# A graph network on one core: segment sums transposed unmerged, messages in partition quarters, each block added at its own base

## What is computed

```python
W   = (edge_attr @ ew + eb).reshape(E, 16, 16)      # 8 features an edge
msg = einsum('ei,eio->eo', x[src], W)
agg = segment_sum(msg, dst, num_segments=N)         # N = 12500
h   = agg + x @ rw + rb
```

## Time and profile before

| | before |
|---|---|
| median of three runs | 7843.1 us |
| profiled execution | 7844.6 us, span 7842.8 us |
| mean granted TensorE clock | 0.978 |
| TensorE matmuls busy | 94% |
| DVE busy | 75% |
| POOL busy | 68% |
| ScalarE busy | 64% |

### The profile page before, as it was taken

One profiled execution on the slowest core, in us unless ns is written; L12 is line 12 of the kernel. 1 busy time (PEld: TensorE's weight loads), 2 busy tenths in 40 slices (PEclk: granted clock), 3 DMA queues, 4 the chain that ended last, 5 costly groups with the idle time before them and its releaser, 6 DMA issues.

```text
span 7842.8 us, 135584 instructions
## 1 busy us (share of the span) xinstructions
PE 7377.1 (94%) x51692; PEld 6562.7 (84%) x51692; DVE 5875.9 (75%) x7566; ACT 5020.2 (64%) x8367; POOL 5324.6 (68%) x5635
## 2 busy tenths in 40 slices
PE   4999999999999899999999999999999999999998
PEld 2888888888888688888888888868888888888887
DVE  3777777777777677777777777767777777777775
ACT  3666666666666466666666666656666666666665
POOL 4677777777777377777777777737777777777772
PEclk7999999999999799999999999989999999999998
DMA  7111111111111111111111111111111111111110
GB/s 37 29 30 30 30 30 30 30 30 30 30 28 29 26 30 30 28 30 30 30 30 30 30 30 30 29 25 29 30 30 30 30 27 30 30 30 30 30 30 20
DMA packets 783265, 229.16 MB, mean 29 GB/s; under 512 B 643869, under 2 KB 733869, under 8 KB 782619
## 3 DMA queue, kind: packets, MB, share of 16 engines
q1 hardware_dynamic: 529252, 172.27, 10.7%
q0 software_dynamic: 180000, 46.44, 6.9%
q10 hardware_dynamic: 73367, 1.76, 1.0%
HBM read 216.52 MB, written 3.52 MB: 28 GB/s over the span
## 4 chain that ended last, share of the span: by engine, by line
PE 66%; ACT 28%; issue 2%; DVE 2%; DMA 1%; DVEq 1%; ACTq 0%
PE bank L1074 57%; ACT distance L914 13%; ACT low_hot L918 13%; PE bank L1088 2%; PE bank L1030 2%; PE bank L1089 2%; ACT z L878 1%; PE bank L1097 1%; PE bank L1098 1%; DMA key_all<-in_src 1%; PE bank L1143 1%; DVE xbig L638 1%; PE bank L1155 1%; DVEq L719 0%; DVE agg L724 0%
## 5 line engine op out<-in xcount | busy, mean ns | idle before, releaser
L468 POOL DMA_INDIRECT xg<-node_table,idx x5625 | 5323.8, 946 | 2394.5 <-issue 1768.1
L1074 PE MATMUL bank<-nodes,low_hot 128*128 128x400 f32 x30000 | 5729.9, 348 | 25.0 <-DVE nodes L651 15.1
L1074 PEld LDWEIGHTS bank<-nodes,low_hot 128*128 128x128 f32 x30000 | 5401.4, 188 | 285.0 <-issue 254.8
L914 ACT ACTIVATE distance<-key_all,low_id 128x640 bf16<-128x640 int16 x3000 | 2242.6, 818 | 2056.8 <-issue 1298.9
L683 DVE TENSOR_TENSOR spread<-mask,bank 128x400 f32<-128x400 uint8 x3750 | 2015.5, 565 | 1571.9 <-PE bank L1074 1571.6
L918 ACT ACTIVATE low_hot<-distance,one 128x640 fp32r<-128x640 bf16 x3000 | 2231.0, 815 | 0.0
L688 DVE TENSOR_REDUCE xg<-spread 128x80 f32<-128x2000 f32 x750 | 1677.3, 2236 | 25.7
L638 DVE TENSOR_TENSOR xbig<-xg,bank 128x1280 f32<-128x1280 f32 x750 | 1327.4, 1810 | 1.0 <-issue 0.2
L1041 PE MATMUL bank<-xbig,hot 128*32 128x144 f32 x18750 | 992.6, 294 | 0.0
L1041 PEld LDWEIGHTS bank<-xbig,hot 128*32 128x32 f32 x18750 | 819.7, 109 | 163.6 <-issue 101.3
L1088 PEld LDWEIGHTS bank<-merge,z 128*128 128x128 f32 x942 | 146.7, 188 | 428.2 <-ACT z L878 422.8
(11 more groups left out here) (109 smaller groups left out, 1031.3 us busy)
## 6 DMA issues: line engine op xcount, KB each, us to landing
key_all<-edge_keys SPq DMA_DIRECT2D x375, 320.0 KB, 3.7
xg<-node_table,idx POOLq DMA_INDIRECT x5625
ea<-in_edge_attr SPq DMA_DIRECT2D x375, 100.0 KB
idx<-in_src SPq DMA_DIRECT2D x375, 7.5 KB
node_table<-rows_room SPq DMA_DIRECT2D x3, 781.2 KB
xbig<-node_table SPq DMA_DIRECT2D x9, 192.0 KB
xbig<-in_x SPq DMA_DIRECT2D x2, 781.2 KB
xbig<-in_dst ACTq DMA_DIRECT2D x1, 782.5 KB, 68.1
```

The costliest lines, as they stand in the source:

```text
L468: pool.indirect_dma_start(out=xg[u][:, j, :], out_offset=None, in_=table[:, :], in_offset=bass.IndirectOffsetOnAxis(ap=idx[u][:, j:j + 1], ...
L914: nc.scalar.activation(distance[f][:, 0:tiles.stop - tiles.start, :], key[u % KEYS][:, tiles, :], ACT.Abs, bias=low_id[:, f:f + 1]).then_i ...
L1074: last = nc.tensor.matmul(p_sel[t % BANKS], low_hot[:, f, t, :], nodes[i][:, f, :, :].rearrange("p d f -> p (d f)"), start=(f, i) == (0, 1 ...
```

## The change

SPAN, SHIFTS, `slide`, `merge`, `set_merges` and the semaphore `s_merge` go, and with them the steps at the start that moved the bases of a round's blocks together. Each block keeps its own base.

```diff
-            base_4 = base_f[:].rearrange("p (r c) -> p r c", c=GANG)
...
-            nc.vector.tensor_copy(base_i[:], base_4[:, :, 0])
...
-            step(nc.vector.tensor_tensor(base_f[:], base_f[:], apart_f, ALU.subtract))
+            nc.vector.tensor_copy(base_i[:], base_f[:, 0:NB])
```

```diff
-                pe.wait_ge(s_merge, n + 1)
...
-                pe.wait_ge(s_add, layer * R + r - r % QROUNDS + CREDIT)
-                nc.tensor.matmul(p_zT, z[r % PAIR][:, D:D + FD], merge[r % SHIFTS][:], start=True, stop=True)
-                nc.tensor.matmul(p_zxT, z[r % PAIR][:, 0:D], merge[r % SHIFTS][:], start=True, stop=True).then_inc(s_T, 1)
+                pe.wait_ge(s_add, layer * NB + (r - r % QROUNDS) * GANG + CREDIT)
+                nc.tensor.transpose(p_zT, z[r % PAIR][:, D:D + FD], ident[:])
+                nc.tensor.transpose(p_zxT, z[r % PAIR][:, 0:D], ident[:]).then_inc(s_T, 1)
```

```diff
+        p_agg = [bank[2][q % GANG * WIN:q % GANG * WIN + D, q // GANG * P:(q // GANG + 1) * P]
+                 for q in range(QROUNDS)]
...
-                nc.tensor.matmul(to, w_now[:], zT[:, 0:count, :].rearrange("p q w -> p (q w)"), start=True, stop=False)
-                nc.tensor.matmul(to, eb_now[:], zxT[:, 0:count, :].rearrange("d q w -> d (q w)"),
-                                 start=False, stop=True).then_inc(s_mm, 1)
+                for first in range(0, count, GANG):
+                    some = range(first, min(first + GANG, count))
+                    for q in some:
+                        nc.tensor.matmul(p_agg[q], w_now[:], zT[:, q, :], start=True, stop=False)
+                    for q in some:
+                        last = nc.tensor.matmul(p_agg[q], eb_now[:], zxT[:, q, :], start=False, stop=True)
+                last.then_inc(s_mm, 1)
```

```diff
-                rounds = quad_rounds(q)
-                bases = [dve.value_load(base_i[0:1, r:r + 1], min_val=0, max_val=N - 1) for r in rounds]
                 dve.wait_ge(s_mm, layer * QUADS + q + 1)
-                for r, base in zip(rounds, bases):
-                    here = agg[:, bass.ds(base, SPAN)]
-                    dve.wait_ge(s_add, layer * R + r + CREDIT)
-                    nc.vector.tensor_tensor(here, here, p_agg[:, r % QROUNDS, :], ALU.add).then_inc(s_add, 1)
+                for r in quad_rounds(q):
+                    blocks = range(r * GANG, min((r + 1) * GANG, NB))
+                    bases = [dve.value_load(base_i[0:1, n:n + 1], min_val=0, max_val=N - 1) for n in blocks]
+                    for n, base in zip(blocks, bases):
+                        here = agg[:, bass.ds(base, WIN)]
+                        dve.wait_ge(s_add, layer * NB + n + CREDIT)
+                        nc.vector.tensor_tensor(here, here, p_agg[r % QROUNDS][:, n % GANG * WIN:(n % GANG + 1) * WIN],
+                                                ALU.add).then_inc(s_add, 1)
```

```diff
                                          bias=low_id[:, f:f + 1]).then_inc(s_dist, 1)
+                if between is not None:
+                    copy_rounds(layer, between)
                 for f in range(FOLD):
...
-                        if g:
-                            copy_rounds(layer, g - 1)
...
-                            compare_keys(layer, b, u + 2, 1)
-                copy_rounds(layer, G - 1)
+                            compare_keys(layer, b, u + 2, 1, between=g)
+                        else:
+                            copy_rounds(layer, g)
```

More of the change, by code:

```diff
@@ L26 @@
 GANG = 4
-SPAN = 100
-SHIFTS = 4
 QUAD = 4
@@ L62, in gnn_kernel @@
     assert E == G * GE and G == BODIES * SLOTS and FD == P and D * (F + 1) <= 512
-    assert GANG * WIN == P and QROUNDS * SPAN <= 512 and FETCHED % RUN == PICKED % RUN == 0 and NB == BLOCKS * G
+    assert GANG * WIN == P and QROUNDS <= 2 * GANG and FETCHED % RUN == PICKED % RUN == 0 and NB == BLOCKS * G
     assert N == NODE_P * PER and PER == CHUNKS * SUB and CHUNKS % SLOTS == 0 and CN <= 512
@@ L122, in gnn_kernel @@
         dst_rel = sb("dst_rel", [P, NB, RUN], I16)
-        base_i = sb("base_i", [P, R], I32)
+        base_i = sb("base_i", [P, NB], I32)
         base_f = sb("base_f", [P, R * GANG])
-        slide = sb("slide", [P, R])
-        merge = [sb(f"merge{i}", [P, SPAN]) for i in range(SHIFTS)]
         far_i = sb("far_i", [P, 1], I32)
@@ L175, in gnn_kernel @@
         z = [sb(f"z{i}", [P, D + FD]) for i in range(PAIR)]
-        zT = sb("zT", [P, QROUNDS, SPAN])
-        zxT = sb("zxT", [D, QROUNDS, SPAN])
+        zT = sb("zT", [P, QROUNDS, P])
+        zxT = sb("zxT", [D, QROUNDS, P])
         low_c = sb("low_c", [G, BLOCKS])
@@ L208, in gnn_kernel @@
         p_z = [bank[i][:, 0:D + FD] for i in range(PAIR)]
-        p_zT, p_zxT = bank[2][:, 0:SPAN], bank[2][0:D, SPAN:2 * SPAN]
-        p_agg = bank[2][0:D, 0:QROUNDS * SPAN].rearrange("d (q w) -> d q w", w=SPAN)
+        p_zT, p_zxT = bank[2][:, 0:P], bank[2][0:D, P:2 * P]
+        p_agg = [bank[2][q % GANG * WIN:q % GANG * WIN + D, q // GANG * P:(q // GANG + 1) * P]
+                 for q in range(QROUNDS)]
         p_far, p_far_agg = bank[0][0:FAR_WIN, 0:D + FD], bank[1][0:D, 0:FAR_WIN]
@@ L269, in gnn_kernel @@
         s_seg = sem("segments_summed")
-        s_merge = sem("merge_onehot_ready")
         s_z = sem("round_copied")
@@ L559, in _ @@
             step(nc.vector.tensor_copy(base_f[:, GANG * G:NB], bank[2][:, P:P + G]))
-            base_4 = base_f[:].rearrange("p (r c) -> p r c", c=GANG)
-            apart_4 = apart_f.rearrange("p (r c) -> p r c", c=GANG)
-            nc.vector.tensor_copy(base_i[:], base_4[:, :, 0])
[L563 to L571, removed]
-            step(nc.vector.tensor_tensor(base_f[:], base_f[:], apart_f, ALU.subtract))
+            nc.vector.tensor_copy(base_i[:], base_f[:, 0:NB])
             step(nc.vector.tensor_tensor(dst_rel[:], dst_at, base_f[:, 0:NB].unsqueeze(2).to_broadcast([P, NB, RUN]),
@@ L746, in segments @@
                         multiply_fetched(layer, b, u)
-                        set_merges(layer, g)
                         if another:
@@ L757, in segments @@
                 add_quad(layer, QUADS - 1)
-                dve.wait_ge(s_add, layer * R + (R + CREDIT))
+                dve.wait_ge(s_add, layer * NB + (NB + CREDIT))
                 apart(dve)
@@ L897, in copy_segments_far, with compare_keys @@
                         nc.scalar.activation(far_zxT[:], p_farxT, ACT.Copy).then_inc(s_fzT, 1)
-            def compare_keys(layer, b, u, half):
+            def compare_keys(layer, b, u, half, between=None):
                 body = layer * BODIES + b + u // SLOTS
@@ L1095, in messages_of @@
                 pe.wait_ge(s_zT, layer * R + rounds[-1] + 1)
-                to = p_agg[:, 0:count, :].rearrange("d q w -> d (q w)")
-                nc.tensor.matmul(to, w_now[:], zT[:, 0:count, :].rearrange("p q w -> p (q w)"), start=True, stop=False)
-                nc.tensor.matmul(to, eb_now[:], zxT[:, 0:count, :].rearrange("d q w -> d (q w)"),
-                                 start=False, stop=True).then_inc(s_mm, 1)
+                for first in range(0, count, GANG):
[5 more added lines that the diff above has]
+                last.then_inc(s_mm, 1)
             def segment_sums(layer):
```

## The result

The changed kernel takes 8598.3 us (8596.3 to 8600.8) where the kernel before took 7842.5 in runs beside it: a ratio of 1.096 (1.0945 to 1.0983). It is slower, as forecast, and lies in the range; the forecast of 8720 was 122 us too high. The profiled execution of after has a span of 8597.0 us and a mean granted clock of 0.904, against 7842.8 us and 0.978.

The account below looks back on a forecast made before the run. TensorE was taken as the bound, waiting for the z copy and DVE's adds. Per layer +423 +19.8 -98.7 -31.3 -18.6 = +294.2; three layers +882.6, start -4.5, on 7844.6 gave 8722.7, said as 8720 us; range 8540 to 8930.

Parts of the forecast that it names:

- The lump: DVE's 20 loads and 20 adds a quad: the products after them start 13.5 us later, rounds of 3.67 us.
- The clock: TensorE at half clock after waiting for the adds: fifth pick tile 5.2 us after them, making 14.1 us late, not 13.5.
- the merge: Merge one-hots removed from DVE's path between the adds and the first taken tile: about 0.25 us less.
- The transposes: On TensorE, two transposes replace two pairs of merging matmuls: -0.25 us a round, bounds -0.1 to -0.35; -31.3 a layer.
- The moved copy: ScalarE copies z before the one-hots, so TensorE's wait goes: -1.05 us in 94 groups a layer, -98.7 a layer.
- The messages: TensorE's message matmuls in four column quarters: -0.6 us, 31 times, -18.6 a layer; bounds -0.85 to +0.5.
- The layer ends: Last group of each layer, where nothing lies beside the adds and five blocks are left over: +19.8 us.
- The start: Removed steps on the bases at the kernel's start: -4.5 us, once.
- Hidden loads: Rival: DVE's sequencer runs all later loads beside the adds; faster, about 7710 us; chance 0.06.
- The dearer clock: Rival: TensorE's clock stays at half for the longest time seen, about +1.6 us more each, 8870 us; chance 0.12.
- the copy gives nothing back: Rival: another wait, DVE's fifth tile or ScalarE's next half, takes TensorE's 1.05 us; 8970 us; chance 0.08.
- cheaper loads: Rival: DVE's value loads are cheaper than now or partly hidden, midway, 8300 us; chance 0.04.

Follow-up runs that it names:

- copy_only: The kernel before with only the z copy moved between ScalarE's distances and one-hots: 7541.4 us, ratio 0.961.
- copy_unmoved: The changed kernel with the z copy put back at its old place after the one-hots: 8894.7 us, ratio 1.134.
- one_load: The changed kernel with one value load a round instead of four, same 20 adds, sums landing on wrong nodes: 7766.8 us, ratio 0.990.
- many_loads: The kernel before with 20 value loads ahead of its five adds, each base loaded four times and one used: 8820.4 us, ratio 1.124.
- keep_busy_2: The changed kernel with TensorE repeating pick tile 2 eight times while it waits for the adds: 8523.6 us, ratio 1.087.
- loads_early_2: The changed kernel with a quad's 20 value loads placed one by one behind earlier takings of pick tiles, where DVE waits: 7788.2 us, ratio 0.993.
- copy_quarters_2: The kernel before with moved z copy and messages in partition quarters, merging matmuls and five adds kept: 7481.0 us, ratio 0.954; on another chip 12190.6 us.

## Why the prediction was right, and by how much not

**The mechanism** held in each step that makes the change slower: value loads of 0.61 us in a row that nothing covers, DVE's lump of adds, TensorE behind it at the transposes, the clock at half after that. copy_only and copy_unmoved fit 7545 and 8895 to within 4 us, one_load and many_loads each show 0.62 us a load, from either side. Of the signs that the prediction named, the loads are there 1875 times at 300 ns, from the first load of a quad to the end of its last add it is 18.1 us (some 18 were forecast), TensorE's wait is 13.3 us (about 14), and the granted clock behind it is 0.50.

**The lump, +13.5 us: measured +13.08** (last add's start 5.58 to 18.66 us, means of 90 quads). A round is 3.60 us in the mean, 3.55 in the quad shown (4054.25 to 4057.78 and so on in DVE's timeline), instead of 3.67: I let the next load begin 0.08 us after the last add began, and it begins after 0.03; from that load to the next add it is 2.61 us where I had 2.65. The last add of round one comes 0.37 us earlier than I said, since the 0.35 us for a long first load, read in one quad, isn't the rule. In the kernel before the same quad misled me the other way: over all quads its first add starts at 4.04 us, in the quad that I read at 4.33. These two slips nearly cancel, which is luck. One quad was taken for all.

**The clock: forecast +0.6 us after 0.25 for the merge, measured 14.27 against 13.69, +0.58**, and by keep_busy_2 0.84 for the clock less 0.26 for the merge one-hots, both as forecast. In the quad shown it is granted 0.50 and 0.82 behind the wait:

```profile
4056.50:4069.60 13.10, 0.19 (x2) 0.00 (x0) 2.96 (x17) 1.27 (x3) 9.99 (x11) 0.60 0.24 41
4069.60:4072.00 2.40, 2.30 (x8) 2.24 (x9) 2.40 (x2) 0.42 (x2) 1.79 (x3) 0.50 0.08 6
4072.00:4074.00 2.00, 2.00 (x11) 1.99 (x10) 2.00 (x4) 0.00 (x0) 1.42 (x2) 0.82 0.07 6
```

Both together: +13.67 instead of +14.1 a quad, 40 us in all.

**The transposes, -0.25 us a round: measured about -0.48** (copy_only 18.01, after 17.54). This is the largest miss, and outside the bounds that I gave, -0.1 to -0.35. I took 0.11 us for each of the two from the earlier trace rows; the pair takes 0.13 together. In the timeline of after the second starts 0.10 us behind the first (4019.74 to 4019.84), and the picks only 0.03 behind the second. So the five transposes of L997 were the right row for the first of the pair and the wrong one for the second, which has 16 stationary columns; why it is so short no run shows. By 94 rounds on the path and the second rounds of 31 groups that is 0.23 x 125 x 3, some 86 us, of the 122.

**The moved copy, -1.05 us:** 1.06 and 1.03. **The messages, -0.6:** -0.55 (1.87 to 1.32). **The layer ends:** +17 to +20 us each where each was to cost +19.8. **The start:** -7.0 us to the first sums, forecast -4.5.

The two large misses, 40 and 86 us, have the same sign, and the small ones nearly cancel, so the sum is off by 122 us. The range held since it reached 180 us below the forecast, though the term of the transposes lay outside its own bounds.

**The rivals.** Hidden loads fell (the lump is in sight; loads_early_2 shows that they can be hidden, by another place in the program, not by the sequencer). The dearer clock fell in after (14.27, no quad over 15.09), but many_loads pays 1.3 us a quad for it. That the copy gives nothing back fell to copy_only, and cheaper loads fell to the 0.62 us of one_load and many_loads. The price of about 200 ns for a register load on the page "Runtime: NRT & Kernel Launch" of the Trainium skill, section "Instruction fetch mechanics", isn't that of these loads: here, from SBUF, 300 ns is the median of 1875, and all but one are under 330 ns.

## What to carry to other kernels

Count the register loads of a dynamic address as path, not as nothing: 0.61 us each here, more than the 0.31 of the add that uses it, unless they stand where their engine waits or works on something long. A step on an engine that is 70% busy can cost all of its time when a buffer ties the bound engine to its last instruction. And a change of several parts deserves to be split: one line of this one (the copy's place) was worth 4%, with the message quarters and with early loads, which weren't part of it, 5.7%. The transposes gave some 0.5 us a round, five rounds a quad, and the twenty adds with their loads, which came with them, put off the last add by 13.1 us a quad.

## What the runs showed of the hardware

- A wait of TensorE of 4 us costs more than one of 13. From the last add to the next sums it is 14.71 us in one_load (mean wait 3.95 us), 14.94 in loads_early_2 (3.9), 14.99 in many_loads (9.4) and 14.27 in after (13.3); without a fall of the clock it is 13.43, or 13.69 in a kernel that has the merge one-hots, as many_loads has. So the clock's price isn't in proportion to the pause. What it follows is how long the clock is still at half once the wait is over, by the trace's records of the granted clock: 5.6 us in one_load, 6.1 in loads_early_2, 5.1 in many_loads and 4.6 in after. In one_load the clock is at half for 6.8 us a quad, most of it behind the wait, in after for 14.1 us, most of it within the wait. In each of the four runs the way grows by 0.43 to 0.46 us with each us of it. An estimate from that line and the 13.43: in after the first 2.8 us at half clock cost nothing, since there DVE sets the pace anyway.
- A 32-bit transpose of a whole 128x128 block and one of 16 stationary columns behind it cost TensorE 0.13 us in a stream of picks, where multiplying the same by a matrix of 100 columns cost 0.57 (timelines of after and before).
- Messages in partition quarters save 0.75 us a quad at 100 columns a round (20.77 to 20.02 us a group, copy_only to copy_quarters_2) and 0.55 at 128 (1.87 to 1.32 us in the timelines).
- The kernel before took 7843 to 7846 us beside all other runs and 11488 on that one chip, where the trace of copy_quarters shows TensorE waiting 2836 us for nothing that the profile names, in the sums.
